# Two images through a convolution and an attention block: the convolution as band matrices for both images at once, and minus the maxima by four 32-row tiles

## The reference, cut to what matters

```
h = group_norm1(x)                                   # mean and variance over all of an image
f = dwconv(h, w3, b3) + dwconv(h, w5, b5) + dwconv(h, w7, b7)   # one kernel per channel, padded
g = sigmoid(gate_w f + gate_b)                       # 1x1
x = x + proj_w (f * g) + proj_b
h = group_norm1(x)
q, k, v = 1x1 convolutions of h                      # N = 9216 pixels, 64 channels
out = softmax(q^T k / 8) v                           # attention over all pixels
return x + out
```

## Time and profile before

| | |
|---|---|
| median of three runs | 3034.27 us |
| the profiled execution | 3029.67 us, its span 3027.9 us |
| mean granted clock of TensorE | 0.986 of 2.4 GHz |
| PE busy | 2883.5 us (95%) |
| DVE busy | 2666.0 us (88%) |
| ACT busy | 2179.2 us (72%) |
| POOL busy | 2237.5 us (74%) |

### The profile page before, as it was taken

The page is one execution under the profiler, slowest core; times in us unless marked ns, Lnnn a source line. Parts: engine busy times, 40 slices in busy tenths (PEclk is TensorE's granted clock), DMA queues, the critical chain, the costliest instruction groups (busy, mean ns, idle before and its releaser), DMA issues.

```text
span 3027.9 us, 56969 instructions
## 1 busy us (share of the span) xinstructions
PE 2883.5 (95%) x20913; PEld 984.0 (32%) x20913; DVE 2666.0 (88%) x3096; ACT 2179.2 (72%) x2442; POOL 2237.5 (74%) x1754
## 2 busy tenths in 40 slices
PE   5878999999999999999997899999999999999998
PEld 2323333333333333333332333333333333333332
DVE  8577899999999999999987899999999999999994
ACT  1156677777777777777764678888888888888887
POOL 1045999999999999999996466666666666666666
PEclk9889999999999999999998999999999999999999
DMA  1020000000000000000001100000000000000000
GB/s 38 3 72 8 8 10 10 10 10 10 10 10 10 10 10 10 10 10 10 8 5 26 24 8 10 10 10 10 10 10 10 10 10 10 10 10 10 10 12 4
DMA packets 30978, 37.16 MB, mean 12 GB/s; under 512 B 6896, under 2 KB 29936, under 8 KB 30064
## 3 DMA queue, kind: packets, MB, share of 16 engines
q1 hardware_dynamic: 30704, 33.56, 4.6%
HBM read 9.94 MB, written 9.44 MB: 6 GB/s over the span
## 4 chain that ended last, share of the span: by engine, by line
PE 75%; DVE 7%; issue 7%; POOL 5%; ACT 4%; DMA 1%; SPq 0%; POOLq 0%; ACTq 0%; DVEq 0%
PE ps L949 32%; PE ps L940 29%; PE ps L956 10%; POOL accA L413 5%; DVE mxp L714 4%; PE ps L1045 3%; DVE ps L730 1%; ACT E L490 1%; ACT tapped L536 1%; PE ps L972 0%; ACT QQ L589 0%; DVE accB L737 0%; PE ps L1125 0%; ACT QS L520 0%; DVE ps L727 0%
## 5 line engine op out<-in xcount | busy, mean ns | idle before, releaser
L413 POOL TENSOR_TENSOR accA<-accA,E 128x512 f32<-128x512 f32 x1224 | 1574.5, 1286 | 458.9 <-ACT E L490 384.3
L490 ACT ACTIVATE E<-ps,bnd 128x1024 f32<-128x1024 f32 x1296 | 1391.0, 1110 | 566.4 <-PE ps L940 469.8
L714 DVE TENSOR_REDUCE mxp<-ps 128x1 f32<-128x1024 f32 x1296 | 1573.8, 1218 | 215.8 <-PE ps L956 191.8
L949 PE MATMUL ps<-E,x 128*64 128x512 f32 x5184 | 1268.2, 605 | 0.5 <-ACT pvb L500 0.5
L940 PE MATMUL ps<-QS,KK 64*128 64x512 f16 x7776 | 1056.4, 377 | 14.0 <-ACT mseed L521 10.1
L730 DVE TENSOR_TENSOR ps<-ps,E 128x512 f32<-128x512 f32 x1260 | 869.0, 690 | 46.6 <-ACT E L490 46.3
L956 PE MATMUL ps<-KK,QM 64*128 64x512 f16 x2592 | 500.8, 383 | 20.7 <-DVE mxp L714 17.6
L940 PEld LDWEIGHTS ps<-QS,KK 64*128 64x128 f16 x7776 | 374.0, 94 | 437.2 <-ACT E L490 24.8
L427 POOL TENSOR_TENSOR f<-f,tapped 128x576 f32<-128x576 f32 x356 | 505.3, 1420 | 0.0
L949 PEld LDWEIGHTS ps<-E,x 128*64 128x64 f32 x5184 | 310.8, 136 | 550.5 <-issue 394.9
L940 PE MATMUL ps<-QS,one 64*128 64x512 f16 x1980 | 377.4, 377 | 0.0
(11 more groups left out here) (105 smaller groups left out, 855.6 us busy)
## 6 DMA issues: line engine op xcount, KB each, us to landing
QS<-QQ SPq DMA_DIRECT2D x144, 64.0 KB, 2.0
x_scratch<-x SPq DMA_DIRECT2D x4, 1152.0 KB, 13.2
QM<-QQ SPq DMA_DIRECT2D x72, 64.0 KB, 2.0
xst<-x_scratch SPq DMA_DIRECT2D x72, 64.0 KB, 2.2
out<-ot SPq DMA_DIRECT2D x72, 64.0 KB, 2.0
xs<-in_x SPq DMA_DIRECT2D x2, 720.0 KB, 8.8
xs<-in_x SPq DMA_DIRECT2D x2, 648.0 KB, 5.9
xs<-in_x SPq DMA_DIRECT2D x2, 576.0 KB, 10.8
```

The source lines that it names most:

```text
L413: nc.gpsimd.tensor_tensor(accA[:, n % 2, :], accA[:, n % 2, :], e, ALU.add).then_inc(adda_free, 1)
L490: nc.scalar.activation(flat(E[:, slot_of(n % 2, p), :, :]), flat(ps[:, S_BANK + 2 * buf:S_BANK + 2 * buf + 2, :]), ACT.Exp, scale=bnd[:, 6 ...
L714: nc.vector.reduce_max(flat(mxp[:])[:, v:v + 1], flat(ps[:, bank:bank + 2, :]), AX.X).then_inc(mx_free, 1)
L949: a = nc.tensor.matmul(ps[C * t:C * t + C, ACC_BANK, :], V[:, t, p, :], E[:, slot_of(par, p), t, :], start=(p == 0), stop=(p == NPAIR - 1) ...
```

## The change

1. The host hands in the images also as rows: four windows of 30 rows (24 and a border of 3) on four groups of 32 partitions, with all channels and columns in the free dimension (`x_rows`), and the conv weights laid out by row of the kernel (`conv_w`).
2. PE builds, for each channel and each horizontal tap, a band matrix of 30 rows by 24: 24 + 2 float32 matmuls of 448 columns, copied by ACT (`take_bands`). A mask row carries the bias.
3. Both images are convolved at the start (`convolve`): 8 sets of 8 channels; for each, 7 horizontal taps on 16 tiles, 448 instructions of 192 columns (96 of each image). DVE copies a set out (`take_convolved`), SP stores it to memory and fetches it into the layout of `f`. Image 1's part is fetched during the attention of image 0.
4. Taps on ACT, POOL and DVE, `hp`, the folding and the padding are gone. POOL takes two small operations of each block in image 0 as it did in image 1.
5. `seed`, `mseed` and the one-row term of `scores` are gone. `minus_maxima` puts the minus maxima of two pairs into four banks by four matmuls of 32 rows each, at the head of the iteration, before the visit. It waits for both exponentials.

```diff
-            def scores(par, p, peers, seeds=None):
+            def minus_maxima(par, p, peers):
                 if peers is not None:
-                    pe.wait_ge(e_ready, peers + 1)
+                    pe.wait_ge(e_ready, peers + 2)
+                for u in (0, 1):
+                    for t in (0, 1):
+                        at = GRP * (2 * u + t)
+                        nc.tensor.matmul(ps[:, S_BANK + 2 * ((p + u) % 2) + t, :], one16[at:at + GRP, :],
+                                         QS[at:at + GRP, par, 2, :], start=True, stop=False, tile_position=(at, 0),
+                                         skip_group_check=True)
+
+            def scores(par, p):
                 keys = slice(p * P, (p + 1) * P)
-                terms = ((KH[:, keys], 0), (KL[:, keys], 0), (KH[:, keys], 1), (one16[:], 2))
-                if seeds is not None:
-                    pe.wait_ge(seeded, seeds)
-                    terms = terms[:3]
-                for k, (of, part) in enumerate(terms):
+                for k, (of, part) in enumerate(((KH, 0), (KL, 0), (KH, 1))):
...
-                    visit(p)
                     if p + 2 < NPAIR:
                         if p == ROW_SUMS + 2 and not first:
                             pe.wait_ge(rs_copied, n)
-                        scores(par, p + 2, n0 + p + 1)
-                        scores(par, p + 3, n0 + p + 2, seeds_before(b, j, p + 4) if is_seeded(b, p + 3) else None)
+                        minus_maxima(par, p + 2, n0 + p + 1)
+                        visit(p)
+                        scores(par, p + 2)
+                        scores(par, p + 3)
                     elif looks:
-                        pe.wait_ge(m_ready, 2 * n + 4)
+                        pe.wait_ge(m_ready, n + 2)
+                        minus_maxima(1 - par, 0, n0 + p + 1)
+                        visit(p)
                         pe.wait_ge(qs_in[1 - par], staged)
-                        scores(1 - par, 0, n0 + p + 1)
-                        scores(1 - par, 1, n0 + p + 2)
+                        scores(1 - par, 0)
+                        scores(1 - par, 1)
...
+            for i in range(BAND_GROUPS):
+                if i >= 2:
+                    pe.wait_ge(bands_out, i - 1)
+                for k in range(BAND_ROWS):
+                    a = nc.tensor.matmul(ps[:, 4 * (i % 2) + k, 0:TAP_COLS],
+                                         shifts[0:K_ROWS, BAND_ROWS * i + k, :, :].rearrange("p g i -> p (g i)"),
+                                         wsum[0:K_ROWS, :], start=True, stop=True)
+                a.then_inc(bands_ps, 1)
...
+            def convolve(s):
+
+                pe.wait_ge(xr_ready, NSET + s + 1)
+                if s >= 2:
+                    pe.wait_ge(conv_out, s - 1)
+                for k in (0, 1):
+                    for dx in range(KW):
+                        for g in range(WINDOWS):
+                            rows = slice(GRP * g, GRP * g + GRP)
+                            for h in range(COLS):
+                                c = CSET * s + COLS * k + h
+                                a = nc.tensor.matmul(
+                                    ps[GRP * h:GRP * h + WROWS, 4 * (s % 2) + g, k * B * W:(k + 1) * B * W].rearrange(
+                                        "p (b x) -> p b x", b=B),
+                                    bands[rows, c * KW + dx, :], xr[rows, :, c, dx:dx + W],
+                                    start=(dx == 0), stop=(dx == KW - 1), tile_position=(GRP * g, GRP * h))
+                a.then_inc(conv_ps, 1)
...
+            def put_convolved(s):
+
+                sp.wait_ge(conv_out, s + 1)
+                for k in range(COLS):
+                    sp.dma_start(f_dram[s, k].rearrange("(g r) k b x -> r g (k b x)", g=WINDOWS),
+                                 evac[GRP * k:GRP * k + WROWS, s % 2, :, :]).then_inc(f_out[s % 2], 16)
+
+            def get_convolved(b, s):
+
+                for half in (0, 1):
+                    for k in (0, 1):
+                        c = C * half + CSET * s + COLS * k
+                        sp.dma_start(f[c:c + COLS, :].rearrange("c (y x) -> c y x", x=W),
+                                     f_dram[s, :, HR * half:HR * half + HR, k, b, :]).then_inc(f_in, 16)
...
+                if b + 1 < B:
+                    sp.wait_ge(v_ps, NCH * (b + 1))
+                    for s in range(NSET):
+                        get_convolved(b + 1, s)
```

More of the change, by code:

```diff
@@ L35 @@
 H_ACT = 4
[L37 to L40, removed]
+KW = 7
+PAD = KW // 2
+WINDOWS, GRP = 4, 32
+WROWS = H // WINDOWS
+WIN = WROWS + 2 * PAD
+MASK_ROW = WIN
+XW = W + 2 * PAD
+COLS = 4
+CSET = 2 * COLS
+NSET = C // CSET
+QUARTERS = 4
+BAND_ROWS = 3
+BAND_GROUPS = WROWS // BAND_ROWS
+TAP_COLS = C * KW
+BETA_ROW, BIAS_ROW = 32, 39
+K_ROWS = BIAS_ROW + 1
 AHEAD = 4
@@ L44, with program @@
 RECS = 4
[L45 to L66, removed]
 QK_TOP = 2.0 ** 14
 ONE = 2.0 ** 14
-M_ROW = 1.0 / (ONE * 64)
-def program(nc, x, per_channel, gate_w, proj_w, q_w, k_w, v_w, out):
+M_ROW = 1.0 / (ONE * GRP)
+def program(nc, x, x_rows, conv_w, per_channel, matrices, out):
     with ExitStack() as ctx:
@@ L542, in attend @@
                     exponentials(n, p)
-                    if p + 2 < NPAIR and is_seeded(b, p + 2):
-                        seed(b, j, p + 2)
                     if p == 1 and j:
@@ L850, in x1_stats @@
+            row_stats(0)
+            weight_norms()
+            row_stats(1)
+            for s in range(NSET):
+                take_convolved(s)
+            for b in range(B):
                 def x1_stats(c):
@@ L938, in scores @@
+            def scores(par, p):
+                keys = slice(p * P, (p + 1) * P)
+                for k, (of, part) in enumerate(((KH, 0), (KL, 0), (KH, 1))):
                     for t in (0, 1):
                         rows = slice(C * t, C * t + C)
[L940 to L942 removed]
+                        a = nc.tensor.matmul(ps[:, S_BANK + 2 * (p % 2) + t, :], of[rows, keys], QS[rows, par, part, :],
+                                             start=False, stop=(k == 2), skip_group_check=True)
@@ L1066, in _ @@
+            for s in range(NSET):
+                convolve(s)
+            pe.wait_ge(conv_out, NSET)
             for b in range(B):
@@ L1070, in gate @@
                     n = NCH * b + c
-                    if b == 0:
-                        pe.wait_ge(f_added, next(k for k in range(CCH + 1) if CROW0[k] * W >= (c + 1) * CH))
                     if c >= 3:
@@ L1155 @@
     raw = {n.removeprefix("L0_conv_"): np.asarray(a) for n, a in inputs.items()}
-    both = ("n1_g", "n1_b", "n2_g", "n2_b", "b3", "b5", "b7", "gate_b", "proj_b", "v_b", "q_b", "k_b")
+    both = ("n2_g", "n2_b", "gate_b", "proj_b", "v_b", "q_b", "k_b")
     columns = [np.tile(raw[n], 2)[:, None] for n in both]
-    columns += [np.tile(raw[n].reshape(C, -1), (2, 1)) for n in ("w3", "w5", "w7")]
-    given = {"x": raw["x"], "per_channel": np.concatenate(columns, axis=1)}
-    given.update({n: raw[n] for n in ("gate_w", "proj_w", "q_w", "k_w", "v_w")})
+    rows = np.zeros((B, P, C, XW), np.float32)
+    for g in range(WINDOWS):
+        first = max(0, WROWS * g - PAD)
+        last = min(H, WROWS * g - PAD + WIN)
+        to = GRP * g + first - (WROWS * g - PAD)
+        rows[:, to:to + last - first, :, PAD:PAD + W] = raw["x"][:, :, first:last, :].transpose(0, 2, 1, 3)
+    conv_w = np.zeros((2, KW + 1, 4, C, KW), np.float32)
+    for i, k in enumerate((7, 5, 3)):
+        o = (KW - k) // 2
+        conv_w[:, o:o + k, i, :, o:o + k] = raw[f"w{k}"][:, 0].transpose(1, 0, 2)
+        conv_w[1, KW, i, :, PAD] = raw[f"b{k}"]
+    for i, n in enumerate(("n1_g", "n1_b")):
+        conv_w[i, 0:KW, 3] = raw[n][None, :, None]
+    matrices = np.stack([raw[n] for n in ("gate_w", "proj_w", "v_w", "q_w", "k_w")], axis=1)
+    given = {"x": raw["x"].reshape(B, C, N), "x_rows": rows, "conv_w": conv_w.reshape(2, KW + 1, 4, TAP_COLS),
+             "per_channel": np.concatenate(columns, axis=1), "matrices": matrices}
     arrays, args = {}, []
```

468 lines of the change are left out of this document (195 added, 273 removed).

## The result

The changed kernel took 3135.05 us (median of 4 runs, 3131.36 to 3139.64); the kernel before, measured beside it, 3032.11 us. The ratio is 1.0341, with a 95% interval of 1.032 to 1.0362. Forecast were 3105 us, in a range of 3030 to 3168, so +71 us over the kernel before, where +103 was measured.

The account below looks back on a forecast made before the run. PE bounds attention, with visits held 1.73 us apart by DVE's reduction. Terms -14 - 8 + 18 - 8 + 86 + 2 = +76 us on 3029.67 give 3106; predicted median 3105 us, range 3030 to 3168.

Parts of the forecast that it names:

- The bound of the iteration: Attention, both images: DVE's reduction keeps visits 1.73 us apart, PE stands 0.21 us, an iteration takes 4.25 us.
- x: Time of the four-tile minus-maxima step ahead of the first visit: 0.34 us, from 0.217, 0.11 and 0.01 for weight loads.
- Two of its signs: Attention: PE idle about 0.2 us before the second visit, and PE's busy share lower than in the kernel before.
- Rival (b): Attention: visits nearer together than 1.73 us, so PE doesn't stand; 129 us less, 2977 us; chance 0.03.
- Rival (a): Minus step: no drain between row counts, four tiles fit one step, x = 0.22; 78 us less, 3028 us; chance 0.14.
- rival (c): Minus step: four tiles run as two pairs, x = 0.54, 3234 us; 3170 at a step and a half; chance 0.12 for both.
- The blocks: Attention: a block takes 18 x 4.25 + 1.0 = 77.5 us; 17 blocks add 18 us in image 0, 86 in image 1.
- Between the attention of image 0 and image 1: Gates to first scores of image 1, 87.44 us before: no change forecast; the same stretch of image 0: -8 us.
- The start: Everything until f is complete and image 0's gates start: 144 us instead of 158.29, -14 us (-33 to +3).
- Gates after 165 us: Sign that the prediction is wrong: image 0's gates starting later than 165 us, with f forecast at 144 us.
- The convolution: PE at the start, from 49 us: 3584 pairs of 192 columns in 85 us, between 66 and 102.
- Rival (d): Start binds: a convolution pair takes 57 ns, 204 us for the convolution, +119 us, 3224 us; chance 0.04.

Follow-up runs that it names:

- 128-row run: Changed kernel with the matmuls that build the band matrices contracting over all 128 partitions instead of 40: 3125.14 us, ratio 1.0317 to the kernel before.

## Why the prediction was right, and where it wasn't

*The bound of the iteration: right.* Forecast was x + 1.73 + 2.18 with x = 0.34, measured 0.32 + 1.72 + 2.19. Two of its signs were ill chosen: PE doesn't show as idle for 0.2 us at the second visit, and its busy share in the attention of image 0 rose (98.8 to 99.2%), since a matmul's way through the array counts as busy and covers the stand. The stand is seen in the starts and in the weight loads. That DVE's reduction is the reason at the second visit is shown by halving it and by moving the visit. Rival (b), visits nearer than 1.73 us, is out as long as the reduction has its length; with the reduction halved they were 1.52 us apart.

*The price of x: right, and both its terms.* A step of 0.217 (doubling it added 0.22) and 0.11 for the change of shape. The row-only change in the earlier trace rows had the right price. Rival (a), no drain, and rival (c), four tiles as two pairs, are out. The Trainium skill (TensorEngine Tiling (Array Packing), Key Properties) says that a change of tiling mode drains TensorE; the runs agree for 32 against 64 rows in that the change costs 0.11 us. Its 3.07 times for four row tiles (TensorE: Matmul & The Clock Gate, Measured speedup vs the span model) doesn't hold in a running stream here: four more matmuls cost what two 64-row ones do, 0.22 us, the full four times. (The prediction's 0.11 us for it was worked out from a matmul's length of 0.38 us; from the step of 0.217 it would have been 0.07.) Not in the prediction is what the place costs: ahead of the visit the step pays one change of shape and nothing of it is free; between the visits it pays two, and the kernel is 56 us faster.

*The blocks: right in sign, a little high.* A block is 76.87 us instead of 77.5; of the 1.0 us above the iterations 0.73 is left (76.87 - 18 x 4.23), and x was 0.02 too large. That makes 20 us over both images too many (+84 measured, +104 forecast).

*Between the attention of image 0 and image 1: 5 us missed.* Before, PE stood 7.12 us for POOL's last taps, and its first four gate instructions then took 3.75 us. After, PE doesn't stand ahead of them, and they take 1.91, which is 1.8 of the 5.2 us. I had counted the wait and not that the clock was low behind it: over the whole stretch the granted clock was 0.85 before and is 0.91 after. Whether that is all of the 5.2 us isn't shown. In image 0 the same stretch gave 5.2 us where 8 were forecast.

*The start: wrong, by 55 us.* The forecast had f ready at 144 us, at most 161, and the gates start at 199.6. "Gates after 165 us" was one of the prediction's own signs of being wrong, and it came. This is the mis-sized term, and it is why the whole is 30 us above the forecast. Its parts, by the forecast's own steps:

- The bands were to be ready at 37 us with passes of 0.39 us after a cold start. They took 0.745 us a pass to the end, PE in the last group until 54.7, ACT's copy of it another 3.5 us. The term was taken from rows at the upper clock; the 128-row run shows the other level to be the reason, and what it costs: 10 us of the whole, since ACT's copies bind next. Those copies I had not costed at all: 3.53 us for 1344 columns.
- Normalization of image 0 took 7.5 us, 1 more than forecast, but began at 60.4, and the root of image 1 at 67.78 and eight small DVE operations ran behind it. The convolution began at 70.7 instead of 49.
- The convolution took 109 us, not 85. The upper bound of the forecast (102, at the fastest pair rate seen) was the better reading, and even that was exceeded, since instructions come in bursts with stalls between. The Trainium skill has 25 ns from matmul to matmul at the least (TensorE: Matmul & The Clock Gate, Wait — 56ns, not 53.3ns?); the trace has 18 ns in bursts over several tiles and 30 with the stalls.
- The tail from the last matmul to the gates was 20 us, not 10: DVE's copy 1.76, then SP's queue, which from 181.46 to 194.4 issues the last stores and eight fetches, two sets' worth, before the last data land.

The timeline of that tail; SPq is the queue of SP:

```profile
179.67 1.76 DVE L704 COPY arena<-ps 128x1536 f32<-128x1536 f32 x1 [11.59 <-PE ps L1021]
181.46 2.19 SPq L281 DMA_DIRECT2D f_scratch<-arena  x4
183.70 10.72 SPq L289 DMA_DIRECT2D f<-f_scratch  x8
```

Rival (d) is out: a pair took 30 ns, not 57, and at the lower level of the clock 32.6. The convolution missed its forecast by 24 us, not by 119. Errors partly cancelled: the sum came to 3105 with the start forecast 55 us too short and everything behind it 25 us too long. That the total lies inside the range is thus in part luck. The range had about 20 us for the start; with the other terms right the total would have been 3160, just inside its upper end.

## What to carry to other kernels

Before work is taken off the bound engine, measure the least distance that its consumers ask between two of its instructions: here visits can't be nearer than 1.73 us, so PE work between them is free up to that, and the same work placed ahead of them isn't. Each change of array shape costs 0.11 us beside its step, so a saved step of 0.217 is half eaten by one change and wholly by two. When work moves off an engine, look at what that engine could now do for the bound one: the seeds on ACT, thrown out by this change, were worth 49 us in image 0 once its taps were gone.

## What the runs showed of the hardware

- *The clock behind the records.* The granted clock of the building stage stands as 1.00 in the windows view of the changed kernel, yet its passes run at half rate. The windows view, columns as in the earlier trace rows:

```profile
13.50:54.70 41.20, 40.53 (x56) 17.75 (x56) 14.26 (x43) 26.18 (x9) 0.39 (x1) 1.00 0.45 131
70.73:179.67 108.94, 74.67 (x3584) 52.48 (x3584) 12.31 (x7) 7.63 (x8) 0.00 (x0) 0.88 0.29 58
```

  A pass of 448 columns in 0.745 us is what the lower level (1.2 GHz) makes of the 0.375 seen in the 128-row run. The trace of the changed kernel has its first change of level at 75.5 us, and up to it the view says 1.00 whatever the level is. The convolution's matmuls show it: these are groups of instructions, with the busy time and the mean ns of one, from 70.7 to 75.3 us, where the clock stands as 1.00, from 103 to 109, where it is 0.50, and from 110 to 119.5, where it is 1.00.

```profile
L1021 PE MATMUL ps<-arena 32*24 32x192 f32 x181 | 5.0, 513 | 9.6 <-ACT arena L544 9.6
L1021 PE MATMUL ps<-arena 32*24 32x192 f32 x192 | 5.6, 512 | 1.1 <-issue 1.1
L1021 PE MATMUL ps<-arena 32*24 32x192 f32 x304 | 5.7, 328 | 4.8 <-issue 4.8
```

  So in these traces a 1.00 ahead of the first change doesn't tell the level; a matmul of known length does. With 40 rows the passes stayed slow to the end of the stage; with 128 rows and the same columns they became fast at about 19.8 us, where that trace has its first change of level (19.7). Why is not settled by these runs.
- *Instruction stream.* A stream of weight loads and matmuls ran 128 pairs in 2.29 us and then stalled, 30 ns a pair in all. At the lower level of the clock a pair took 29.6 ns with 96 columns and 32.6 with 192, at the upper one 30.0 with 192. With 384 columns the kernel before had 28.4 ns a pair at its fastest: fewer columns than that bought nothing.
- *Four 32-row tiles* in f16 with 512 columns, writing four PSUM banks, keep the pace of one step (0.22 us for four more).
